# Row maxima of the first attention carried in a spare row of Q instead of by added products

## The reference

```
q = relu(x @ Wq + bq);  k = relu(c @ Wk + bk);  v = relu(c @ Wv + bv)
scores = einsum('bhqd,bhkd->bhqk', q, k) / sqrt(16)
scores = where(query mask, scores, 1e-9)
o = softmax(scores) @ v;  x = layer_norm(o + x)
x = mamba2_block(x)              # projection, conv, scan, gate, out-projection
x = cross_attention(x, c)        # 8 heads of 32
```

## Time and profile before

| | |
|---|---|
| median of three runs | 1339.41 us (1336.35 to 1339.72) |
| the profiled execution: span, first to last instruction | 1337.2 us |
| mean granted clock of TensorE | 0.990 of full speed |
| instructions | 43414 |
| median above the profiled span | 2.2 us |

### The profile page before, as it was taken

The page is one execution under the profiler, slowest core; times in us unless marked ns, Lnnn a source line. Parts: engine busy times, 40 slices in busy tenths (PEclk is TensorE's granted clock), DMA queues, the critical chain, the costliest instruction groups (busy, mean ns, idle before and its releaser), DMA issues.

```text
span 1337.2 us, 43414 instructions
## 1 busy us (share of the span) xinstructions
PE 1291.6 (97%) x15624; PEld 1148.0 (86%) x15624; DVE 1208.1 (90%) x3056; ACT 1130.8 (85%) x3407; POOL 928.7 (69%) x1200
## 2 busy tenths in 40 slices
PE   5879999999999999999999999999999999999987
PEld 4668889988888998889998889989888898888875
DVE  6789999999999999999999999999999989999982
ACT  5658989888889988888988888998888898888875
POOL 3366777777767777777777776777777777766774
PEclk9889999999999999999999999999999999999999
DMA  6102221212221112222121222211222221111110
GB/s 203 40 34 72 69 77 38 70 56 69 77 77 62 52 49 69 77 77 77 38 66 60 69 77 77 61 53 50 69 77 77 71 71 34 62 56 57 49 57 25
DMA packets 41283, 87.00 MB, mean 65 GB/s; under 512 B 5744, under 2 KB 10992, under 8 KB 41072
## 3 DMA queue, kind: packets, MB, share of 16 engines
q1 hardware_dynamic: 40208, 83.81, 19.7%
q10 hardware_dynamic: 864, 0.42, 0.1%
HBM read 75.53 MB, written 8.68 MB: 63 GB/s over the span
## 4 chain that ended last, share of the span: by engine, by line
PE 87%; DVE 4%; ACT 4%; issue 2%; DMA 1%; POOL 1%; SPq 1%; ACTq 0%; DVEq 0%
PE bank L319 26%; PE bank L422 10%; PE bank L550 6%; PE bank L412 5%; PE bank L379 5%; PE bank L533 5%; PE bank L436 4%; PE bank L564 4%; PE bank L669 4%; PE bank L360 3%; PE bank L604 3%; PE bank L625 2%; PE bank L654 2%; PE bank L470 2%; PE bank L416 1%
## 5 line engine op out<-in xcount | busy, mean ns | idle before, releaser
L951 DVE SCALAR_TENSOR_TENSOR ACC<-bank,cw,ACC 128x250 f32<-128x250 f32 (+2 forms) x576 | 264.1, 462 | 5.9 <-ACT ACC L1535 3.3
L319 PE MATMUL bank<-xnT,wnl 128*128 128x256 f32 x640 | 201.6, 315 | 3.3 <-DVE xnL L883 2.3
L1622 ACT ACTIVATE PC<-bank,stc 128x128 f32<-128x128 f32 x512 | 182.5, 389 | 7.7 <-DVE stc L1068 4.3
L319 PE MATMUL bank<-xnL,wnh 128*128 128x256 f32 x640 | 180.3, 282 | 0.0
L319 PE MATMUL bank<-xnT,wnh 128*128 128x256 f32 x640 | 179.8, 281 | 0.0
L800 DVE TENSOR_REDUCE sta<-bank 128x4 f32<-128x512 f32 x256 | 163.7, 673 | 7.8 <-PE bank L379 7.5
L977 DVE TENSOR_TENSOR_SCAN L<-DB,id 128x1024 f32<-128x1024 f32 x64 | 146.8, 2293 | 0.8 <-DMA DB<-dec_scratch 0.8
L319 PEld LDWEIGHTS bank<-xnT,wnl 128*128 128x128 f32 x640 | 121.9, 190 | 26.0 <-issue 17.6
L1437 ACT ACTIVATE PTA<-bank 128x512 f32<-128x512 f32 x256 | 133.3, 628 | 9.0 <-PE bank L416 5.3
L1916 POOL TENSOR_TENSOR PC<-PC,stc 128x512 f32<-128x512 f32 x128 | 132.1, 1042 | 11.3 <-DVE stc L1075 11.3
L319 PEld LDWEIGHTS bank<-xnL,wnh 128*128 128x128 f32 x640 | 122.4, 191 | 0.0
(11 more groups left out here) (210 smaller groups left out, 4709.9 us busy)
## 6 DMA issues: line engine op xcount, KB each, us to landing
DB<-dec_scratch SPq DMA_DIRECT2D x64, 512.0 KB, 4.0
cT<-in_cT SPq DMA_DIRECT2D x64, 256.0 KB, 2.6
xT<-in_xT SPq DMA_DIRECT2D x32, 256.0 KB, 4.0
xt<-in_xt SPq DMA_DIRECT2D x32, 256.0 KB, 3.8
out_x<-X SPq DMA_DIRECT2D x32, 256.0 KB, 4.0
QM<-qm_rows SPq DMA_DIRECT2D x32, 128.0 KB, 4.1
XC<-in_win SPq DMA_DIRECT2D x2, 644.0 KB, 6.7
PTC<-in_wout SPq DMA_DIRECT2D x2, 256.0 KB, 6.6
```

Source lines behind the costliest of these rows:

```text
L319: mm = e.matmul(t[:, c0:c0 + T], wt[:, k, m:m + 128], x[:, k, :], start=(n == 0), stop=(n == 5))
L951: e.scalar_tensor_tensor(out=w, in0=t[:, 0:T].rearrange("p (b t) -> p b t", b=NB)[:, :, 0:125 + k], scalar=cw[:, c, k:k + 1], in1=w, op0=A ...
L1622: op = e.activation(PC[n % 4][:, p, :], t[:, p * 128:(p + 1) * 128], ACT.Exp, bias=stc[g % 4][:, 4 * i + p:4 * i + p + 1], accum_out=stc[g ...
```

## The change

The negated maxima are no longer added by a product. QT now holds each of the two masked copies of Q, as KT did for K: [128, 2, 2, 256] instead of [128, 2, 256]. In copy 0 the rows of the second head are zero, and so the row 16 of each 32 is spare; in copy 1 it is row 0. KT gets a one in that row, through its bias. So the score product over 32 partitions adds to the score whatever stands in the spare row of Q: nothing for sA, the negated maximum for sT.

- qe makes two copies with a scale and a bias, and qm multiplies both (512 columns instead of 256).
- sA has 16 products of 128 columns instead of 8 of 256. mA writes its results in the order copy, row group, m.
- nm, nw, the f32r split and NT go. tn transposes the 16 columns of `sta`, nt_ copies 16 rows once to TM, and SP moves them to the spare rows by two transfers of eight rows (put), for which sT waits.
- sT loses its four products with ones.
- The lists of all engines and USES are new. In PE's loop there is one call of everything as before. put(g+3,1) stands behind dec_out(g+2) and put(g+4,0) behind both dec_in(g+2).
- load_x(0), load_c(0), lo_x(0) and lo_c(0), calls without work for group 0, leave the lists.

```diff
+        qb = sb("qb", [128, 2, 2])
-        QT = ring("QT", 2, [128, 2, T])
+        QT = ring("QT", 2, [128, 2, 2, T])
-        NM = ring("NM", 2, [128, 4, 32], F32R)
-        NT = ring("NT", 2, [128, 4, 128], F32R)
+        TM = ring("TM", 2, [16, 128])
...
+            def put(g, b):
+                if ok(g):
+                    e.wait_ge(s_nt_, 2 * g + b + 1)
+                    for i in range(2):
+                        e.dma_start(QT[g % 2][16 - 16 * i::32, :, i, b * 128:(b + 1) * 128],
+                                    TM[b][8 * i:8 * i + 8, :]).then_inc(d_tm[b], 16)
...
+            for g in range(NG - 7):
+                dec_out(g + 2)
+                put(g + 3, 1)
+                dec_in(g + 2, 0)
+                dec_in(g + 2, 1)
+                put(g + 4, 0)
+                load_u(g + 2)
+                load_t(g + 4)
+                load_m(g + 6)
+                load_x(g + 6)
+                store(g)
                 load_c(g + 6)
...
-                    for m in range(2):
+                    for i in range(4):
                         for j in range(4):
                             r = slice(32 * j, 32 * j + 32)
-                            mm = e.matmul(ts[j][:, m * 256:(m + 1) * 256], QT[g % 2][r, m, b * 128:(b + 1) * 128],
-                                          KT[g % 2][r, m, b, :, :], start=True, stop=True)
+                            mm = e.matmul(ts[j][:, i * 128:(i + 1) * 128], QT[g % 2][r, i // 2, i % 2, b * 128:(b + 1) * 128],
+                                          KT[g % 2][r, i // 2, b, i % 2, :], start=True, stop=True)
...
-                    e.wait_ge(s_nw, ns + 1)
-                    e.transpose(t[:, 0:128], NM[ns % 2][:, :, :].rearrange("p j i -> p (j i)").bitcast(F32), ident[:, :]).then_inc(s_tn, 1)
+                    e.wait_ge(s_mA, 4 * ns + 4)
+                    e.transpose(t[0:16, 0:128], sta[ns % 4][:, 0:16], ident[:, :]).then_inc(s_tn, 1)
...
-                    e.wait_ge(s_nt_, ns + 1)
+                    e.wait_ge(d_tm[b], 32 * g + 32)
                     for i in range(4):
                         for j in range(4):
                             r = slice(32 * j, 32 * j + 32)
-                            e.matmul(ts[j][:, i * 128:(i + 1) * 128], KT[g % 2][r, i // 2, b, i % 2, :],
-                                     QT[g % 2][r, i // 2, b * 128:(b + 1) * 128], start=(i == 0), stop=False)
-                    for j in range(4):
-                        r = slice(32 * j, 32 * j + 32)
-                        mm = e.matmul(ts[j][:, :], onesr[r, :], NT[ns % 2][r, :, :].rearrange("p i q -> p (i q)"),
-                                      start=False, stop=True)
+                            mm = e.matmul(ts[j][:, i * 128:(i + 1) * 128], KT[g % 2][r, i // 2, b, i % 2, :],
+                                          QT[g % 2][r, i // 2, i % 2, b * 128:(b + 1) * 128], start=True, stop=True)
...
-                e.tensor_scalar(kb[:, i, :], pc[:, 2:4], par[:, i:i + 1], None, ALU.mult).then_inc(z_sq, 1)
+                e.tensor_scalar(qb[:, i, :], pc[:, 0:2], par[:, i:i + 1], None, ALU.mult)
+                e.tensor_scalar(kb[:, i, :], pc[:, 2:4], par[:, i:i + 1], sel[:, 3 + i:4 + i], ALU.mult, ALU.add).then_inc(z_sq, 1)
...
-                    e.activation(QT[g % 2][:, m, :], t[:, 0:T], ACT.Relu, bias=pc[:, m:m + 1]).then_inc(s_q, 1)
+                    for i in range(2):
+                        op = e.activation(QT[g % 2][:, m, i, :], t[:, 0:T], ACT.Relu, bias=qb[:, i, m:m + 1], scale=par[:, i:i + 1])
+                    op.then_inc(s_q, 1)
...
-                        e.wait_ge(s_sT, ns - 1)
+                        e.wait_ge(d_tm[b], 32 * g)
                     e.wait_ge(s_tn, ns + 1)
-                    for i in range(4):
-                        op = e.activation(NT[ns % 2][:, i, :], t[:, 0:128], ACT.Copy, scale=sel[:, 3 + i:4 + i])
-                    op.then_inc(s_nt_, 1)
+                    e.activation(TM[b][:, :], t[0:16, 0:128], ACT.Copy).then_inc(s_nt_, 1)
...
-                    e.tensor_tensor(QT[g % 2][:, m, :], QT[g % 2][:, m, :], QM[g % 2][:, :], ALU.mult).then_inc(s_qm, 1)
+                    e.tensor_tensor(QT[g % 2][:, m, :, :], QT[g % 2][:, m, :, :],
+                                    QM[g % 2][:, :].unsqueeze(1).to_broadcast([128, 2, T]), ALU.mult).then_inc(s_qm, 1)
```

More of the change, by code:

```diff
@@ L308, in sync @@
[L308 to L310 removed]
+            load_x(1); load_m(0); load_m(1); load_t(0); load_c(1); load_x(2); put(0, 0); load_c(2); put(0, 1)
+            put(1, 0); load_x(3); put(1, 1); dec_out(0); load_m(2); load_c(3); dec_in(0, 0); dec_in(0, 1); load_m(3)
+            load_x(4); load_t(1); load_u(0); load_c(4); put(2, 0); put(2, 1); load_m(4); load_m(5); dec_out(1)
@@ new lines, in sync @@
+            load_x(5); dec_in(1, 0); dec_in(1, 1); load_t(2); load_t(3); load_u(1); put(3, 0); load_c(5)
+            for g in range(NG - 7):
[9 more added lines that the diff above has]
+                store(g)
+                load_c(g + 6)
+            dec_out(NG - 5); put(NG - 4, 1); dec_in(NG - 5, 0); dec_in(NG - 5, 1); put(NG - 3, 0); store(NG - 7)
@@ new lines, in sync @@
+            load_u(NG - 5); load_x(NG - 1); dec_out(NG - 4); put(NG - 3, 1); load_m(NG - 1); load_c(NG - 1)
+            load_t(NG - 3); dec_in(NG - 4, 0); dec_in(NG - 4, 1); put(NG - 2, 0); load_t(NG - 2); load_u(NG - 4)
+            dec_out(NG - 3); put(NG - 2, 1); dec_in(NG - 3, 0); dec_in(NG - 3, 1); load_u(NG - 3); put(NG - 1, 0)
+            dec_out(NG - 2); load_t(NG - 1); store(NG - 6); put(NG - 1, 1); dec_in(NG - 2, 0); dec_in(NG - 2, 1)
+            load_u(NG - 2); dec_out(NG - 1); dec_in(NG - 1, 0); dec_in(NG - 1, 1); load_u(NG - 1); store(NG - 5)
@@ new lines, in gpsimd @@
+            nr(3, 1); yl(2, 0); dx(2, 1); s2_(2, 0); qm(5, 0); qm(5, 1); ga(2, 1); r2(2, 0); yl(2, 1); s2_(2, 1)
+            r2(2, 1); lo_u(2); nC(1, 0); nC(1, 1); nC(1, 2); hr(2, 0); nC(1, 3); hr(2, 1)
+            for g in range(2, NG - 5):
+                dx(g + 1, 0)
+                xr(g + 2, 0)
+                lo_x(g + 4)
+                xd(g + 1, 0)
+                xr(g + 2, 1)
+                rs(g + 2, 0)
+                lo_c(g + 4)
+                rs(g + 2, 1)
+                nr(g + 2, 0)
+                nr(g + 2, 1)
+                ga(g + 1, 0)
+                xd(g + 1, 1)
+                s2_(g + 1, 0)
+                yl(g + 1, 0)
+                dx(g + 1, 1)
+                ga(g + 1, 1)
+                r2(g + 1, 0)
+                qm(g + 4, 0)
+                yl(g + 1, 1)
+                s2_(g + 1, 1)
+                nC(g, 0)
+                hr(g + 1, 0)
+                nC(g, 1)
+                qm(g + 4, 1)
+                r2(g + 1, 1)
+                lo_u(g + 1)
+                hr(g + 1, 1)
+                nC(g, 2)
+                nC(g, 3)
```

985 lines of the change are left out of this document (428 added, 557 removed), and 22 rows, old and new, of the table USES.

## The result

The changed kernel takes 1432.97 us (median of four runs, 1429.33 to 1436.18) against 1338.53 for the kernel before: a ratio of 1.071, 95% interval 1.0684 to 1.0737. I had said 1327 and a range up to 1346. The profiled execution has a span of 1427.5 us, 90.3 more than before.

A forecast was written before the change was run, and what follows sets the result against it. The prediction took PE's work to bound the loop. Products -14.7, sA +1.3, order on PE -4.8, wait for put +3 and fill +3 summed to -12.2 us: 1327 us, range 1312 to 1346.

The forecast's parts named there:

- So in the loop nothing ever makes PE wait, and a microsecond taken from PE is a microsecond of the period: Loop, PE busy for all 39.48 us of a period: its savings count fully until DVE's 36.7 us or a wait.
- The products, -14.7: On PE, dropping the four products with ones from each of 64 sT saves 0.23 us each time, 14.7 us.
- The order on PE: PE's loop has 12 runs of plain f32 work between f32r projections instead of 13: 4.8 us less.
- PE's busy time falling by under 10 us: Sign on PE that the forecast is wrong, named beside a period above 39.2 us.
- hidden under PE both ways: ACT: qe doubles to at most 74 us from some 30, net at least 15 us less, costing PE nothing.
- 35 us more, in POOL's 10 us of idle time a period: POOL: qm on 512 columns instead of 256, 64 x 0.54 us more, covered by idle time.
- The wait for put, +3: Second sT on PE waits for SP's transfers: a stall of 0.1 us in 28 periods, 3 us.
- (b): Rival, slower: the second sT waits for put in every period; 1346 us at a landing of 3.1; chance 0.13.
- Fill, +3: First two groups: four steps from transpose to sT take 3.7 us instead of 2.7, less nm and nw: 3 us more.
- Drain, "I take nothing": Last 80 us, without first attention: the new order may give or take 3 us, counted as nothing.
- (d): Rival: in sT the four products with ones were hidden in the drain of the scores; 1342 us, chance 0.06.
- (c): Rival: the decay chain from bd makes y wait for lg, half a microsecond late; 1338 us, chance 0.12.

The follow-up runs named there:

- e14: The kernel before without the four products with ones of each sT, NT still made, order unchanged: 1336.3 us, ratio 0.9990.
- e15: The kernel before with qe's step done twice on ACT, the second time into unused columns: 1345.2 us, ratio 1.0054.
- e9: The old arithmetic in the changed kernel's new orders and banks, nm and nw directly behind the last maxima of a half: 1446.2 us, ratio 1.0807.
- e7: The changed kernel with split_x (ACT) and lo_x (POOL) much earlier, and nC ahead of hr with its reciprocals earlier on DVE: 1383.6 us, ratio 1.0340.
- e12: e11 without qe's masked copy of Q for the odd head blocks from the third group on: 1374.8 us, ratio 1.0267.
- e11: The new arithmetic in the kernel before's orders, tn(g,0) in another bank, oa earlier on ACT, puts ahead of load_x: 1388.3 us, ratio 1.0373.
- e1: The changed kernel with the split of x on ACT and lo_x on POOL moved long before they are needed: 1412.2 us, ratio 1.0567.
- e17: The kernel before without the products with ones, and with oa(g,0) ahead of th(g-1,3) on ACT: 1334.1 us, ratio 0.9965.
- e2: The changed kernel with lo_x moved two steps up on POOL, ahead of dx and xr: 1454.0 us, ratio 1.0866.

## Why the prediction was wrong, step by step

- **"So in the loop nothing ever makes PE wait, and a microsecond taken from PE is a microsecond of the period"**: the failed reading. PE did not wait, but that did not make its work the bound. As I now read it, the period before is that of a cycle over several engines (scores, PTA's copy, av, OA's copy, o, q, qe, q1, y, the maxima, the scan), in step with PE and as long as its work. Taking PE's share of it away gave 0.0 us a period (e14), and 1 us on ACT gave 0.24 (e15). The cycle itself is my reading; its links were not tested one by one.
- **The products, -14.7**: their size on PE was read rightly (0.23 us each), their worth was some 1 us in the old orders. It can be more in the new ones, where the whole new arithmetic brings 13 us (e9 to after), the products and all else together.
- **"The order on PE", -4.8, and the moved steps on POOL**: the step that made the loss. I counted the runs of plain f32 work on PE and the steps behind put on SP, and did not cost the moved steps of POOL at all: lo_x behind nC, dx and xr, nC behind hr. The runs showed in its place a wait of PE for xL, 51.0 us in 27 times, behind POOL's run from nC to xa and the scan. With the old arithmetic the new orders cost 108 us (e9); moving back two of POOL's steps, with what they need on ACT and DVE, brings 49 (e7). My own sign of being wrong, PE's busy time falling by under 10 us, shows it too: it rose by 21.8, from 1291.6 to 1313.4.
- **Nothing of the scan against POOL**: the rows before show no case, as POOL is idle when the scan begins (the trace has one, cL at 1.92 us, that I had not read); I should have asked which instructions the new list puts beside it. It makes the scan's 2.28 us into 2.7 in the mean, and 0.73 into 2.70 for an xa that it holds (13 of 64).
- **qe, "hidden under PE both ways"**: hidden on ACT's idle time, not on the cycle. 0.97 us more a group; 8.2 us in the kernel before (e15), some 14 in the old orders with the new arithmetic (e12).
- **POOL, "35 us more, in POOL's 10 us of idle time a period"**: qm measured 1.29 us, as read. The idle time was there, but not in the run from nC to XH that the period waits for.
- **The wait for put, +3, rival (b)**: 4.1 us in six places. The size is near, but not for my reason: I had 0.1 us in every period, and it was 1.5 us in five places between 300 and 1100 us and once 2.6 in the fill. The issues on SP took 0.53 us in the median and not 0.33 (0.55 with the step to the next and not 0.37), and nothing shows put's landing. It never decided.
- **sA +1.3**: 1.10 us in the chain, as taken; **tn**: 0.11 us in both kernels, nothing, as taken.
- **Fill, +3**: 3.9 measured, but of other parts: with the old arithmetic the new orders cost 6.5 (e9, first wp at 180.9), and the new arithmetic gives 2.7 back.
- **Drain, "I take nothing"**: +15.2. The last seven periods take 226.6 us with the new orders alone (e9, 19.0 more than before), 216.4 with the new arithmetic in the old orders (e11, 8.8 more) and 223.9 in e7. No run was made on its inside; open.
- **"Slower" had 0.14**, nearly all of it (b) and half of (d). (c), y waiting for lg, appears behind the real cause (12.9 us in e1). The chance for a wait on POOL was none, because the argument stopped at idle time.

Open are the 45 us that e7 still has above the kernel before, and what holds the old orders with the new arithmetic at 40.77 us: qe is about 0.4 of the 1.2 (e12), the rest was not found. The new banks were not tested apart from the new orders. No version tried that keeps the maxima beats the kernel before (e17 leaves them out); the best of the changed one is e7, at 1.034 (1.0321 to 1.0358).

## What to carry to other kernels

In a loop whose order is written out for every engine, cost each moved step in the list of each engine that it is on, and name what stands behind it there; idle time elsewhere in the period pays for nothing. An engine that is busy for the whole period isn't shown to be the bound by that: leave out a little of its work in one run, and see whether the period follows. When a wait is found, look for the next chain of about its length before pricing its removal: 51 us of waiting were worth 21.

## What the runs showed of the hardware

- DVE's scan with two inputs in SBUF and POOL's two-input steps exclude each other in both directions: 2.28 becomes 3.18 us behind DX, 3.00 behind xL; 0.73 becomes 2.70 (xa), 1.04 becomes 3.03 (XH), 1.26 becomes 2.06 in the mean (xL in e2). The kernel before has it too: 24 of 31 cL take 1.94 us in the mean in place of 1.29.
- Behind 10 of the 27 waits for xL, all of them 1.88 to 2.18 us long, TensorE's products went from 0.28 to 0.41 us and a block of 1.09 us to between 1.66 and 1.98, at a granted clock of 0.96 in the stages read; behind the other 17, ten of them as long, the block took 1.09 to 1.18. With the shorter waits of e1, 0.6 us in the mean, the clock of its stages is 1.00.
- An issue on SP of the small transfers between SBUF tiles takes 0.53 us in the median of 128 (0.52 to 0.67); the three others of the earlier trace rows take 0.33.
